# A graph layer's gather split between GpSimd and SyncE: one tile in 64 fetched row by row from register addresses

## What is computed

```python
for l in range(2):
    W = jnp.einsum('rb,bio->rio', coeffs[l], bases[l])
    h = jnp.einsum('ni,rio->rno', x, W)
    msg = h[edge_type, src] * deg_inv[dst][:, None]
    agg = jax.ops.segment_sum(msg, dst, num_segments=num_nodes)
    x_new = agg + x @ self_loops[l]
    if l < n_layers - 1:
        x_new = jax.nn.relu(x_new)
    x = x_new
```

## Time and profile before

| | us |
|---|---|
| three executions | 3428.5, 3435.57, 3437.17 |
| median | 3435.57 |
| span of the profiled execution, from its first to its last instruction | 3411.3 |
| start-up stage, until the first gather | about 357 |
| first layer, its gathers | 357 to 1707 |
| second layer, its gathers | 1783 to 3090 |
| experts, to the end | about 3150 to 3411 |
| GpSimd busy in the span | 1649.4 (48%) |
| TensorE busy in the span | 2398.6 (70%) |
| TensorE's mean granted clock | 0.814 |

### The profile page before, as it was taken

One profiled execution on the slowest core, in us unless ns is written; L12 is line 12 of the kernel. 1 busy time (PEld: TensorE's weight loads), 2 busy tenths in 40 slices (PEclk: granted clock), 3 DMA queues, 4 the chain that ended last, 5 costly groups with the idle time before them and its releaser, 6 DMA issues. The chain is left out here.

```text
span 3411.3 us, 37691 instructions
## 1 busy us (share of the span) xinstructions
PE 2398.6 (70%) x9525; PEld 1737.8 (51%) x9528; DVE 1074.1 (31%) x3125; ACT 626.8 (18%) x1391; POOL 1649.4 (48%) x1712
## 2 busy tenths in 40 slices
PE   6999357777777777776882766666666666566287
PEld 3788235555555555554561544444444444455065
DVE  3787022222222222222220333333233333234233
ACT  4455101111111111110120011111111211110033
POOL 0000655555555555555506555555655555551645
PEclk9999678888888888888895877777777777788587
DMA  8764433334333333433423332333332223231531
GB/s 225 250 232 192 139 100 123 128 125 133 123 124 124 126 124 125 128 122 112 131 90 93 88 91 87 88 87 88 91 88 84 86 87 90 85 87 32 164 110 54
DMA packets 159887, 397.24 MB, mean 116 GB/s; under 512 B 34926, under 2 KB 92241, under 8 KB 145932
## 3 DMA queue, kind: packets, MB, share of 16 engines
q0 software_dynamic: 81648, 219.65, 22.1%
q10 hardware_dynamic: 35772, 124.12, 9.4%
q1 hardware_dynamic: 42337, 51.93, 5.5%
HBM read 260.70 MB, written 138.94 MB: 117 GB/s over the span
## 5 line engine op out<-in xcount | busy, mean ns | idle before, releaser
L515 POOL DMA_INDIRECT gnn_ring<-table,g_idx x1564 | 1512.7, 967 | 1418.2 <-PE gnn_pagg L558 680.0
L558 PE MATMUL gnn_pagg<-gnn_ring,gnn_oh 128*128 x3904 | 1215.4, 460 | 483.7 <-issue 427.0
L558 PEld LDWEIGHTS gnn_pagg<-gnn_ring,gnn_oh 128*128 128x128 f32 x3904 | 838.0, 228 | 886.9 <-issue 759.7
L542 DVE TENSOR_TENSOR gnn_oh<-gnn_col,g_dst 128x256 f32<-128x256 f32 x976 | 408.9, 426 | 1471.2 <-DVEq L49 1214.0
L800 ACT COPY second_wr<-gnn_pm 128x512 f32<-128x512 f32 x196 | 103.0, 597 | 1107.8 <-DMA pre_bs<-in_L_gnn_bases 992.7
L1054 ACT ACTIVATE gnn_qe<-gnn_pq,gnn_bq 128x128 f32<-128x128 f32 x98 | 36.1, 368 | 1078.0 <-remote 1036.1
L402 PE MATMUL pre_psum<-pre_whigh,pre_high 128*128 128x512 f32 x392 | 159.0, 406 | 13.1 <-DVE pre_low L309 8.1
L336 DVE SCALAR_TENSOR_TENSOR second_wr<-pre_bs,pre_cr,second_wr 128x512 f32<-128x512 f32 x232 | 159.5, 748 | 2.8
L744 PE MATMUL gnn_pm<-gnn_whigh,gnn_high 128*128 128x512 f32 x392 | 157.5, 402 | 3.5 <-issue 2.5
L744 PE MATMUL gnn_pm<-gnn_whigh,gnn_low 128*128 128x512 f32 x392 | 153.8, 392 | 6.8 <-issue 6.7
L744 PE MATMUL gnn_pm<-gnn_wlow,gnn_high 128*128 128x512 f32 x392 | 152.9, 390 | 4.2 <-issue 4.2
(11 more groups left out here) (174 smaller groups left out, 2382.6 us busy)
## 6 DMA issues: line engine op xcount, KB each, us to landing
table<-pre_rows ACTq DMA_DIRECT2D x49, 1024.0 KB
table<-second_wr ACTq DMA_DIRECT2D x48, 1024.0 KB
gnn_ring<-table,g_idx POOLq DMA_INDIRECT x1564
bucket<-gnn_zrow SPq DMA_DIRECT2D x16, 650.0 KB
g_xT<-bucket SPq DMA_DIRECT2D x20, 520.0 KB, 6.3
pre_bs<-in_L_gnn_bases SPq DMA_DIRECT2D x32, 240.0 KB
pre_bs<-in_L_gnn_bases SPq DMA_DIRECT2D x30, 256.0 KB
x1T<-gnn_x1T ACTq DMA_DIRECT2D x49, 128.0 KB
```

The source lines that it names most:

```text
L515: eng.indirect_dma_start(self.ring[:, q % RG, t, 0:D], None, self.g.table[self.l][:, :], bass.IndirectOffsetOnAxis(ap=self.g.idx[:, at:at ...
L542: self.nc.vector.tensor_tensor(self.oh[:, h, :, :], self.col[:, :].unsqueeze(1).to_broadcast([P, n, P]), self.g.dst[:, ds(q * TPG + h * n, ...
L558: mm = nc.tensor.matmul(pagg[:, k, 0:self.width], self.oh[:, h, i, :], self.ring[:, ds(q & (RG - 1), 1), t, 0:self.width].rearrange("p o n ...
```

## The change

In both layers 11 tiles, the fourth tile of each group 31, 47, ... 191 (the groups that lie in the ring's last place, without the first of them), are no longer gathered by GpSimd. SyncE fetches their 128 rows one at a time: `rows` loads four row numbers into registers, then issues four DMAs of one row (1 KB) each to one partition of a staging tile `stage`, which has two places. It does so for 8 rows after each counted group, so 128 rows take 16 groups, and the rows of a tile are fetched during the 16 groups before its own. `fill`, after the ninth group of each round of 16, waits until TensorE has left the tile's place in the ring (on `pairs`) and until its 128 rows have landed, and issues one DMA of 128 KB from the staging tile to the ring; SyncE's `count` waits for it before it counts the tile's group. The row numbers of the 11 tiles are made by VectorE in the start-up stage, written to HBM by GpSimd as 11 rows of 128, and loaded by SyncE one row at a time.

```diff
@@ -28,6 +28,9 @@
 NG = -(-NT // TPG)
 NTP = NG * TPG
 RG = 16
+AWAY = RG - 1
+NAWAY = NG // RG - 1
+PER = P // RG
 FREE = 2
 HALF = 2
...
+            eng.wait_ge(away_ok, 1)
+            with nc.allow_non_contiguous_dma(reason="a tile's indices turn from a column into a row"):
+                eng.dma_start(g.away.rearrange("j p -> p j"), away[:, :]).then_inc(away_out, 16)
+            eng.wait_ge(away_out, 16)
...
+                first = (RG + AWAY) * TPG + TPG - 1
+                V.scalar_tensor_tensor(out=away[:, :], in0=srci[:, first:NTP:RG * TPG], scalar=float(R),
+                                       in1=eti[:, first:NTP:RG * TPG], op0=ALU.mult, op1=ALU.add).then_inc(away_ok, 1)
...
+def nc_values(nc, eng, ap):
+
+    return nc.values_load_multi_w_load_instructions(
+        ap, engines=[eng.engine], min_val=0, max_val=NP * R - 1,
+        skip_runtime_bounds_check_because="a row's index is made of a node and a relation")[1]
...
+        self.stage = s.sb("stage", [P, 2, D])
+        self.index = s.sb("index", [1, 2, P], I32)
+        self.index_in = [s.sem(f"index_in{k}") for k in range(2)]
+        self.rows_in = [s.sem(f"rows_in{k}") for k in range(2)]
+        self.filled = s.sem("filled")
...
+    def gathered(self, q):
+
+        return min(TPG, NT - q * TPG) - (q % RG == AWAY and q >= RG)
+
+    def rows(self, eng, q):
+
+        j, lo = q // RG, q % RG * PER
+        if j >= NAWAY:
+            return
+        if lo == 0:
+            eng.wait_ge(self.index_in[j % 2], 16 * (j // 2 + 1))
+        for p in range(lo, lo + PER, 4):
+            at = nc_values(self.nc, eng, self.index[0:1, j % 2, p:p + 4])
+            for i in range(4):
+                eng.dma_start(self.stage[p + i:p + i + 1, j % 2, :], self.g.table[self.l][ds(at[i], 1), :]
+                              ).then_inc(self.rows_in[j % 2], 16)
+
+    def indices(self, eng, j):
+
+        eng.dma_start(self.index[:, j % 2, :], self.g.away[j:j + 1, :]).then_inc(self.index_in[j % 2], 16)
+
+    def fill(self, eng, j):
+
+        slot = eng.value_load(self.g.reuse[0:1, j * RG + AWAY:j * RG + AWAY + 1], min_val=2, max_val=NG + NB)
+        eng.wait_ge(self.pairs, slot)
+        eng.wait_ge(self.rows_in[j % 2], 16 * P * (j // 2 + 1))
+        eng.dma_start(self.ring[:, AWAY, TPG - 1, 0:D], self.stage[:, j % 2, :]).then_inc(self.filled, 16)
+        if j + 2 < NAWAY:
+            self.indices(eng, j + 2)
+
     def count(self, eng, between=None):
 
+        for j in range(2):
+            self.indices(eng, j)
         for q in range(NG):
-            eng.wait_ge(self.landed[q % RG], 16 * sum(min(TPG, NT - p * TPG) for p in range(q % RG, q + 1, RG)))
+            eng.wait_ge(self.landed[q % RG], 16 * sum(self.gathered(p) for p in range(q % RG, q + 1, RG)))
+            if q % RG == AWAY and q >= RG:
+                eng.wait_ge(self.filled, 16 * (q // RG))
             eng.sem_inc(self.groups_in, 1)
             if between:
                 between(q)
+            self.rows(eng, q)
+            if q % RG == RG // 2 and 0 < q // RG <= NAWAY:
+                self.fill(eng, q // RG - 1)
 
     def gather(self, eng):
         for q in range(NG):
@@ -510,7 +571,7 @@
                 last = eng.value_load(self.g.reuse[0:1, q + FREE - 1 - RG:q + FREE - RG], min_val=2, max_val=NG + NB)
                 eng.wait_ge(self.pairs, last)
                 eng.sem_inc(self.gate, 1)
-            for t in range(min(TPG, NT - q * TPG)):
+            for t in range(self.gathered(q)):
                 at = q * TPG + t
                 eng.indirect_dma_start(self.ring[:, q % RG, t, 0:D], None, self.g.table[self.l][:, :],
                                        bass.IndirectOffsetOnAxis(ap=self.g.idx[:, at:at + 1], axis=0)
```

More of the change, by code:

```diff
@@ L103, in __init__ @@
         self.bounds = dram("bounds", (P,), I32)
+        self.away = dram("away", (NAWAY, P), I32)
         self.bucket = dram("bucket", (MAXT * P, ROW), F32)
@@ L163, in startup @@
         idi = s.sb("idi", [P, P], I32)
+        away = s.sb("away", [P, NAWAY], I32)
         cf = s.sb("cf", [4 * NBASE, 4 * R])
@@ L179, in startup @@
         var_ok, std_ok, xn_ok, xT_ps, xT_ok = (s.sem(n) for n in ("var_ok", "std_ok", "xn_ok", "xT_ps", "xT_ok"))
-        bi_ok, bi_out, bound_in = (s.sem(n) for n in ("bi_ok", "bi_out", "bound_in"))
+        bi_ok, bi_out, bound_in, away_ok, away_out = (s.sem(n) for n in ("bi_ok", "bi_out", "bound_in", "away_ok", "away_out"))
         cf_in, w_ps, w_sb = (s.sem(n) for n in ("cf_in", "w_ps", "w_sb"))
```

## The result

The changed kernel takes **3780.15 us** (median of four runs, 3778.65 to 3803.22) where the kernel before took 3436.37 in the same job (four runs, 3428.5 to 3442.12): a ratio of 1.102, 95% interval 1.099 to 1.104. It is 344 us slower. The forecast was 3410 us, with 3520 as the upper end of its range.

The account below looks back on a forecast made before the run. GpSimd's gathers were taken to lie on the path although GpSimd waits. Removing 22 gave -27.5 us, copies and packets +1.5, SyncE's work 0: -26 from 3435.57 gives 3410 us, range 3400 to 3520.

Parts of the forecast that it names:

- The reading of the rounds: GpSimd's rounds of gathers: a round is the gathers' time plus a rest of 6 to 8 us, so gathers bound it.
- The sign that it named: GpSimd's rounds with 15 gathers: about 1.25 us shorter, same rest behind, pace over 172 groups down 0.08 us a layer.
- What the change removes: GpSimd's rounds: 22 gathers fewer, 11 in each layer, at 1.25 us each, 27.5 us less.
- What it adds on SyncE: SyncE after each of 176 groups a layer: loads, address operations, DMA issues, 5.5 us taken, below the pace, cost 0.
- The cover: SyncE's slack of 1.3 to 1.5 us a group, plus its lead as GpSimd runs up to 16 groups ahead of TensorE.
- `fill`'s wait: SyncE waiting for TensorE to leave the ring place: about 45 us, hidden by eight counted groups, 54 us; cost 0.
- the copy and the traffic: 11 copies of 128 KB a layer and more packets beside the gathers: 1.5 us in all, between 0 and 5.
- Start-up: Start-up stage: VectorE's extra operation under 0.3 us, GpSimd writing the row numbers while otherwise idle; cost 0.
- The median's 24.3 us above the span: Whole kernel: the median of executions lies 24.3 above the profiled span, so the forecast starts from 3435.57 us.
- First rival: GpSimd's gathers are hidden, TensorE slow at block starts for its own sake: change gives 0, 3436 us; chance 0.17.
- Second rival: SyncE's row work after each group becomes the bound: at 8 us a group 3672 us; chance 0.14.
- Third rival: DMAs as such hold TensorE, so SyncE's rows in GpSimd's rests do too: 3848 us, or 3452 at a tenth; chance 0.14.

Follow-up runs that it names:

- gone_again: Changed kernel without SyncE's row fetches, copy and wait, so the 22 gathers are left out with nothing in their place; held job: 3406.04 against 3433.61 us, ratio 0.992.
- rows_again: Changed kernel with all 1564 gathers kept, rows fetched to a staging tile nobody reads, no copy or wait for TensorE; held job: 3782.87 us, ratio 1.106.
- after_fourth: The changed kernel itself, unaltered, run again in a clear job: 2586.88 us against 2585.31 for the kernel before, ratio 1.0008.
- gone_only: Changed kernel without SyncE's row fetches, copy and wait, 22 gathers left out with nothing in their place; clear job: 2559.41 against 2585.29 us, ratio 0.9905.
- rows_only: Changed kernel with all 1564 gathers kept, rows fetched to a staging tile nobody reads, no copy or wait for TensorE; clear job: 2590.93 us, ratio 1.003.
- counts_third: Kernel before plus 26 semaphore instructions on SyncE after each of 176 groups a layer, no rows; held job: 3525.3 against 3433.61 us, ratio 1.025.
- hbm_loop: Changed kernel with rows fetched by a loop into an HBM tensor, from which the copy to the ring reads; clear job: 3677.59 against 2584.42 us, ratio 1.422.
- counts_slow: Kernel before plus 26 semaphore instructions on SyncE after each of 176 groups a layer, no rows; clear job: ratio 1.000.

## Why the prediction was wrong

- *The reading of the rounds* (gathers lie on the path although GpSimd waits): right as to the total, gone_again is 27.6 us faster. The sign that it named is shown in part. Between the first burst and the 176th count the rest behind a round is 8.3 and 6.9 us in gone_again's trace against 7.9 and 6.7 in before's, and the pace over 172 groups falls by 0.02 and 0.07 us where 0.08 was forecast for each layer. Two traces are too few to tell such a difference.
- *What the change removes, 27.5 us*: 27.6 in a held job, 25.9 in a clear one.
- *What it adds on SyncE, 4.9 to 6.5 us a group, "so SyncE keeps up and it costs 0"*: **this step failed.** The duration is met where nothing is held, 4.9 us, partly by luck: an issue took 0.32 us and not 0.48, a load 0.63 and not 0.35. It is wrong in a held burst, from some 4 us after its start until about 1.5 us after its end, 17 of the 27 us of a round in before. There the 26 instructions take about 0.7 us each, 18 us a group. What a group cost at the end was a pace of 8.59 us in the first layer and 7.24 in the second. All nearest rows that I took for a price were of the start-up, of stretches without gathers, or of instructions one at a time. The earlier trace rows showed that in a burst two other engines come nearly to a halt with nothing that they wait for. I used this against TensorE and did not ask what it does to SyncE's 26 instructions.
- *The cover, SyncE's lead of up to 16 groups*: wrong. At a layer's start there is no lead, and the longest burst stands there; 112 and 102 us were lost before the 16th count.
- *`fill`'s wait, 0; the copy and the traffic, 1.5*: as forecast within about half a per cent, as far as rows_again beside the changed kernel can tell. But the wait that was worked out, some 45 us for each tile, didn't take place. Below is all that `fill` waited for TensorE in the changed kernel; in the clear job of after_fourth it never waited.
```profile
SPq L549 <- PE gnn_pagg L619: 10.8, 3, 10.3
```
- *Start-up, 0*: not quite. The first gather starts at 358.7 to 362.7 us in the 15 traces of kernels that make the 22 tiles' row numbers and at 356.5 to 357.9 in the five that don't, so the change costs some 1 to 6 us there. In the changed kernel GpSimd's first index work already starts 4.6 us late (124.18 us against 119.56), before any of these numbers exists; why is open.
- *The median's 24.3 us above the span*, which the text ahead of the prediction puts down in part to what lies before the first and after the last instruction: in each run with both numbers that part is 1.7 us (3781.65 and 3779.9). The rest is that the profiled execution was a fast one. The sum doesn't hang on it.
- *First rival* (gathers hidden): refuted by gone_again in a held job; gone_only shows the same for a clear one, where GpSimd never waits. The Trainium skill's rule beside it (SBUF - State Buffer, Who interferes with whom) is that the matmul engine waits on nobody for the memory's ports. In clear jobs the traces agree, with TensorE busy 371 of 400 us beside the gathers. In held jobs TensorE steps slowly beside them, but SyncE's semaphore instructions, which touch no tile, do so too, so these steps are no evidence against a rule on ports.
- *Second rival* (SyncE becomes the bound): this is what came, with its marks as listed: groups landed long before they were counted, TensorE waiting for `groups_in`, GpSimd's waits grown. It had 0.14, and 3672 us at 8 us a group. Its 8 us a group came from no row, and that the mean pace was nearly that, (8.59 + 7.24) / 2 = 7.9, is luck: the cause is the hold and not a slow issue. It gave the second layer more of the loss than the first, 158 against 106 us, where the rounds lost 69 and 249; it lacked the first bursts, 102 and 112, and what came back behind them, 82 and 86.
- *Third rival* (DMAs as such hold TensorE): refuted for a clear job, where rows_only has all the transfers and 1.003. In a held one counts_third has none and still 1.025, and TensorE's idle time in the sum with nothing that the profile shows as its cause is smaller in the changed kernel than in before:
```profile
PE gnn_pagg L558 <- issue: 427.0, 236, 22.5
...
PE gnn_pagg L619 <- issue: 105.4, 99, 10.8
```
  A small share of the transfers in a held job isn't excluded.

What stays open: what makes a job held or clear, and through what the gathers hold the other engines' instructions. The start-up of one kernel takes the same in both within 4 us, DMA packets of the gathers' queue have the same median duration (159 ns), one chip showed both. And I can't say what the first 4 us of a burst, in which SyncE isn't held yet, stand for.

## What to carry to other kernels

When work is moved to an idle engine, price its instructions by rows from the same stretch in which they will run, beside the same neighbours, and count them: 26 short instructions took 5 us in one stretch and 18 in the other. If an engine without a wait shows steps that don't fit its instructions, ask first which other sequencers show them too; an engine that only signals looks idle and may be the next bound. And look at the stage's start apart from its rounds, since a lead that covers everything later isn't there yet.

## What the runs showed of the hardware

- In held jobs, from some 4 us after a burst of GpSimd's indirect DMAs begins until 1.5 to 2.5 us after its end, SyncE starts an instruction about every 0.7 us or a multiple, be it a semaphore increment (0.06 us otherwise), a register operation (0.07), a branch (0.16) or a DMA issue (0.28 to 0.31), in straight code and in loops alike. TensorE's steps of 2.1 us are three times that. In clear jobs nothing of the kind shows: in counts_slow none of SyncE's 9473 steps in the two layers lies between 0.65 and 0.75 us.
- The kernel before takes 2585 us in the one and about 3400 in the other. TensorE's mean granted clock is 0.93 and 0.81. The low mean isn't a mark of a held job by itself: hbm_loop, in a clear job, had TensorE waiting for SyncE and a mean of 0.809.
- A DMA issue with a register as its source row takes 225 ns on SyncE, one with registers on both sides, into HBM, 520 ns. A load of four registers takes 0.55 us in straight code there (0.49 in the changed kernel's held job) and 0.30 in hbm_loop's loop.
